# One-hot tiles for the score passes of a graph network: built on VectorE from row numbers, or transposed once, stored and loaded

## The reference

```
x = _layernorm(x + _L0_gnn_ref(x, edge_index, edge_attr_64, ...), axis=-1)   # three attention layers, 4 heads
x = _layernorm(x + _L1_gnn_ref(x, edge_index, edge_weight, ...), axis=-1)    # two graph convolutions
x = _layernorm(x + _L2_gnn_ref(x, edge_index, ...), axis=-1)                 # one graph convolution
x = _layernorm(x + _L3_gnn_ref(x, src, dst, ...), axis=-1)                   # two mean-aggregation layers
```

```
logits = jax.nn.leaky_relu(a_s[src] + a_d[dst] + ew[:, None], NEG_SLOPE)
m = jax.ops.segment_max(logits, dst, num_segments=n)
ex = jnp.exp(logits - m[dst])
```

## Time and profile before

| | |
|---|---|
| time, 3 runs | 5626.39, 5626.62, 5635.58 us; median 5626.62 |
| profiled execution | span 5076.4 us from its first to its last instruction; median less span is 550.2 us |
| busy share of the span | PE 77%, DVE 75%, ACT 68%, POOL 59% |
| transfers | 1061.18 MB, 209 GB/s over the span |
| score passes | `delta` from 1251.5 to 1611.3, 2041.6 to 2327.3, 2753.6 to 2933.5 and 2959.6 to 3085.1 us |

### The profile page before, as it was taken

The page is one execution under the profiler, slowest core; times in us unless marked ns, Lnnn a source line. Parts: engine busy times, 40 slices in busy tenths (PEclk is TensorE's granted clock), DMA queues, the critical chain, the costliest instruction groups (busy, mean ns, idle before and its releaser), DMA issues. The chain is left out here.

```text
span 5076.4 us, 107540 instructions
## 1 busy us (share of the span) xinstructions
PE 3921.6 (77%) x23992; PEld 2865.7 (56%) x23992; DVE 3818.0 (75%) x14850; ACT 3446.1 (68%) x11317; POOL 3017.8 (59%) x2914
## 2 busy tenths in 40 slices
PE   2999999565997798994998974997876676665554
PEld 1666766344775455773555752444765565665554
DVE  5899999676998787887886966997768787444443
ACT  0899999554886576784776863887878787333332
POOL 2888888475552122661223452887757676767777
PEclk9999999788998899997999997998999898997666
DMA  2566666587997576994776984775766566543332
GB/s 63 162 186 199 199 194 193 175 288 242 351 349 250 180 239 205 338 354 160 233 241 230 350 290 156 225 227 171 230 205 212 189 204 190 155 145 116 93 101 70
DMA packets 606699, 1061.18 MB, mean 209 GB/s; under 512 B 109737, under 2 KB 130875, under 8 KB 606509
## 3 DMA queue, kind: packets, MB, share of 16 engines
q1 hardware_dynamic: 524780, 920.61, 53.0%
q0 software_dynamic: 81728, 138.51, 10.7%
HBM read 608.75 MB, written 453.92 MB: 209 GB/s over the span
## 5 line engine op out<-in xcount | busy, mean ns | idle before, releaser
L2534 POOL DMA_INDIRECT got_c<-table,src_row x980 | 930.4, 949 | 387.6 <-issue 295.6
L1428 POOL DMA_INDIRECT src_got_s<-table,src_row x588 | 554.6, 943 | 452.9 <-PE bank L1474 105.1
L2566 PE MATMUL bank<-pick_c,got_c 128*128 128x128 f32 x1960 | 327.7, 319 | 349.6 <-DMA got_c<-table,src_row 271.2
L2076 PE MATMUL bank<-w_all,dt_m 128*128 128x512 f32 x1176 | 567.7, 599 | 35.0 <-DMA dt_m<-delta_t 33.4
L2566 PEld LDWEIGHTS bank<-pick_c,got_c 128*128 128x128 f32 x1960 | 284.2, 223 | 392.5 <-issue 233.5
L2050 POOL TENSOR_TENSOR part_m<-part_m,half_sum_m 128x512 f32<-128x512 f32 x98 | 158.7, 1619 | 580.3 <-DVE half_sum_m L2283 580.3
L1601 ACT ACTIVATE z_s<-z_s,shift_s,dev_s 128x128 f32<-128x128 f32 x1080 | 444.2, 486 | 1.8 <-DVE shift_s L1739 1.3
L791 PEld LDWEIGHTS bank<-w_mean,ht 128*128 128x128 f32 x2352 | 312.4, 193 | 142.9 <-issue 142.9
L2590 PE MATMUL bank<-w_c,agg_c 128*128 128x128 f32 x1960 | 365.4, 311 | 5.0 <-ACT agg_c L2711 4.7
L2711 ACT COPY agg_c<-bank 128x512 f32<-128x512 f32 x245 | 142.6, 582 | 325.4 <-DVE bank L1914 277.8
L788 PE MATMUL bank<-bias,first_row 128*128 128x512 f32 x588 | 321.8, 629 | 38.7 <-ACT ht L851 13.8
(11 more groups left out here) (352 smaller groups left out, 11925.4 us busy)
## 6 DMA issues: line engine op xcount, KB each, us to landing
table<-rows SPq DMA_DIRECT2D x294, 256.0 KB
x_s<-table SPq DMA_DIRECT2D x270, 256.0 KB
x_c<-table SPq DMA_DIRECT2D x245, 256.0 KB
table<-z_s SPq DMA_DIRECT2D x196, 256.0 KB
table<-z_c SPq DMA_DIRECT2D x196, 256.0 KB
table<-mid_s SPq DMA_DIRECT2D x172, 256.0 KB
own_rows_s<-table SPq DMA_DIRECT2D x147, 256.0 KB
pick_t_s<-picks_t SPq DMA_DIRECT2D x147, 256.0 KB
```

The costliest lines, as they stand in the source:

```text
L1428: nc.gpsimd.indirect_dma_start(out=src_got[r][:, g, :], out_offset=None, in_=tables[l].rows, in_offset=bass.IndirectOffsetOnAxis(ap=src_ro ...
L2076: nc.tensor.matmul(b_h[k % n_h][:, :], dt[b.slot][:, k, :], w_all[:, l, :, :].rearrange("p h d -> p (h d)"), start=True, stop=True).then_i ...
L2534: nc.gpsimd.indirect_dma_start(out=got[r][:, g, :], out_offset=None, in_=t_in.rows, in_offset=bass.IndirectOffsetOnAxis(ap=src_row[:, t:t ...
L2566: ins = nc.tensor.matmul(b_sum[r][:, k * P:(k + 1) * P], got[b.slot][:, k, :], pick[r][:, k, :], start=k == 0, stop=sage, skip_group_check ...
```

## The change

The transposed one-hot tiles are no longer made from `pick` by TensorE and ScalarE, nor stored, nor loaded. In `edge_structure` VectorE writes the keys of all slots as bytes; SyncE stores them in one row of 25088 bytes and loads that row into all 128 partitions (`keys`, 25088 bytes a partition, kept to the end). A new input, `row_of`, holds each partition's number. In every step of `edge_scores` VectorE makes `pick_t` of a batch with one instruction, which compares 512 bytes of `keys` with `row_of`. `pick_t` has two buffers instead of four. GpSimd's pacing in the slot pass waits for `pick` instead of the transposed tile.

```diff
-        picks_t = nc.dram_tensor("picks_t", (nb * P, GB * P), F32, kind="Internal").ap()
+        key_row = nc.dram_tensor("key_row", (1, n_slots), U8, kind="Internal").ap()
...
+        row_of = sb("row_of", [P, 1])
+        keys = sb("keys", [P, n_slots], U8)
+        keys_in = ctx.enter_context(nc.semaphore("keys_in"))
...
-                n_load = 13
+                n_load = 14
...
                         sp.dma_start(iota[:, :], io["iota"]).then_inc(loaded, 16)
+                        sp.dma_start(row_of[:, :], io["row_of"]).then_inc(loaded, 16)
                         sp.dma_start(wet[:, :, :], io["L0_gnn_We"].rearrange("l e h -> e l h")).then_inc(loaded, 16)
                         sp.dma_start(bem[:, :, :], io["be_all"]).then_inc(loaded, 16)
                         sp.wait_ge(iotas, 3)
                         sp.dma_start(row_map.rearrange("(p r) f -> p (r f)", p=P),
                                      map_def[:, :, :].rearrange("p r f -> p (r f)")).then_inc(map_out, 16)
+                        sp.wait_ge(keys_made, 1)
+                        sp.dma_start(key_row[0, :].rearrange("(q e) -> q e", q=rq), key_bytes[:, :]).then_inc(keys_out, 16)
+                        sp.wait_ge(keys_out, 16)
+                        sp.dma_start(keys[:, :], key_row.to_broadcast([P, n_slots])).then_inc(keys_in, 16)
                         sp.wait_ge(map_out, 16)
...
                         st(nc.vector.tensor_tensor(kr[:, :], kr[:, :], sr[:, :], ALU.add))
+                        nc.vector.tensor_copy(key_bytes[:, :], kr[:, :]).then_inc(keys_made, 1)
...
                                 sp.wait_ge(ht_made, b.count(1, 1))
                                 sp.sem_inc(sp_pace, 1)
                                 sp.dma_start(turned_batch(state_t[0], b), ht[r][:, :]).then_inc(ht_stored[r], 16)
-                                sp.wait_ge(pick_t_made, b.count(1, 1))
-                                sp.sem_inc(sp_pace, 1)
-                                sp.dma_start(turned_batch(picks_t, b), pick_t[r][:, :]).then_inc(pick_t_stored[r], 16)
...
                                 elif b > 5 and g == 3:
-                                    pool.wait_ge(pick_t_made, b - 4)
+                                    pool.wait_ge(pick_made, b - 3)
...
                                 nc.tensor.matmul(bank[1][:, :], w_first[:, :], xt[b.half][:, :], start=True,
                                                  stop=True).then_inc(h_made, 1)
-                                pe.wait_ge(pick_made, b.count(1, 1))
-                                hold(pe, pick_t_made, b.count(1, 0))
-                                for g in range(GB):
-                                    ins = nc.tensor.transpose(bank[4][:, g * P:(g + 1) * P], pick[b.slot][:, g * P:(g + 1) * P], ident[:, :])
-                                ins.then_inc(picks_turned, 1)
...
                                 nc.scalar.activation(ht[b.slot][:, :], hidden[r][:, :], ACT.Identity,
                                                      bias=beta_col[:, 0:1]).then_inc(ht_made, 1)
-                                act.wait_ge(picks_turned, b.count(1, 1))
-                                hold(act, pick_t_stored[b.slot], b.ring4(16, -16))
-                                nc.scalar.copy(pick_t[b.slot][:, :], bank[4][:, :]).then_inc(pick_t_made, 1)
...
                                 hold(dve, pick_stored[b.slot], b.ring4(16, -16))
-                                hold(dve, picks_turned, b.count(1, -1))
                                 for k in range(GB):
...
-                src_got, own_rows, pick_t, dt = (fours(n) for n in ("src_got", "own_rows", "pick_t", "dt"))
-                delta = pairs("delta")
+                src_got, own_rows, dt = (fours(n) for n in ("src_got", "own_rows", "dt"))
+                delta, pick_t = pairs("delta"), pairs("pick_t")
...
-                        def load_picks(b):
-                            hold(sp, spread_made, b.count(1, -3))
-                            sp.sem_inc(sp_pace, 1)
-                            sp.dma_start(flat(pick_t[b.slot]), turned_batch(picks_t, b, start)).then_inc(pick_in[b.slot], 16)
...
                         def loads(b):
                             load_own(b)
-                            load_picks(b)
                             if not early(b):
...
                             pe.wait_ge(own_in[r], b.ring4(16))
-                            pe.wait_ge(pick_in[r], b.ring4(16))
+                            pe.wait_ge(picks_made, b.count(1, 1))
                             if first:
                                 hold(pe, dt_made, b.count(1, 0))
                             else:
                                 hold(pe, delta_made, b.count(1, 0))
                             for g in range(GB):
-                                ins = nc.tensor.matmul(b_spread[:, g * D:(g + 1) * D], pick_t[r][:, g, :], own_rows[r][:, g, :],
+                                ins = nc.tensor.matmul(b_spread[:, g * D:(g + 1) * D], pick_t[b.half][:, g, :], own_rows[r][:, g, :],
                                                        start=True, stop=True, skip_group_check=True)
                             ins.then_inc(spread_made, 1)
...
                         dve.wait_ge(banks_open, len(set_by_dve))
+                        dve.wait_ge(keys_in, 16)
...
+                        def build_picks(b):
+                            hold(dve, spread_made, b.count(1, -1))
+                            dve.sem_inc(dve_pace, 1)
+                            nc.vector.tensor_scalar(flat(pick_t[b.half]), keys[:, bass.ds((b.batch() + start) * (GB * P), GB * P)],
+                                                    row_of[:, 0:1], None, ALU.is_equal).then_inc(picks_made, 1)
 
...
                         def step_two(at):
+                            b = at(0)
+                            if b:
+                                build_picks(b)
                             b = at(1)
                             if b:
                                 moments(b, 0)
...
                                 moments(b, 1)
                             b = at(0)
                             if b:
+                                build_picks(b)
                                 residual(b, 0)
                             b = at(1)
                             if b:
...
                                 residual(b, 0)
                                 middle(b, 0)
                                 moments(b, 0)
+                            b = at(0)
+                            if b:
+                                build_picks(b)
                             b = at(1)
                             if b:
                                 set_bias(b, 0)
...
+        "row_of": _np.arange(P, dtype=_np.float32).reshape(P, 1),
```

19 lines of the change are left out of this document (11 added, 8 removed).

## The result

The changed kernel takes 5652.24 us (median of 11 runs, 5641.83 to 5659.17) beside 5640.23 us for the kernel before (11 runs, 5626.39 to 5647.69). The ratio is 1.0025, 95% interval 1.0014 to 1.0035, so +8 to +20 us. The prediction was 5675, +48.5. The direction is right and the size is not: about a quarter of it came. 5652.24 does lie inside the stated range of 5648 to 5710, but by luck: the kernel before measured 13.6 us more in 11 runs than in the three from which the prediction started.

A forecast was written before the change was run, and what follows sets the result against it. VectorE was taken to limit passes 1 to 3 and a VectorE-TensorE loop pass 4; 20.6 + 10.5 + 10.8 + 7.8 - 2 (slot pass) + 0.8 (start) = +48.5, so 5626.6 -> 5675 us, range 5648 to 5710.

The forecast's parts named there:

- The difference, 550.2 us: Whole kernel: median run 5626.6 us minus profiled span 5076.4 us, taken as time outside the span and left unchanged.
- pass 1: First score pass, 49 batches, two-layer order: VectorE is the limit, so each build adds 0.42 us, +20.6 us.
- pass 2: Second score pass, 49 batches, one-layer order: VectorE alone would need 6.11 us against 5.95 a batch, +7.8 us.
- pass 3: Third score pass, 25 batches, two-layer order: VectorE is the limit, 0.42 us a build, +10.5 us.
- pass 4: Fourth score pass, 24 batches, solo order: build lies inside a VectorE-TensorE loop, 0.45 us each, +10.8 us.
- the surplus for collisions and for the register step: Added to the build's 0.40 us: 0.02 for GpSimd collisions, and in pass 4 0.03 for register step and semaphore.
- Loads taken away in passes 1, 3 and 4: Removed 256 KB one-hot loads: nobody waits for them in the steady part, so they give nothing.
- the stall: In pass 2, ScalarE's 33.3 us wait for the score store; 12.6% less traffic ends it, with no further relief.
- A: Build reads bytes at one element a cycle, 0.62 us each: together +78 us, 5704 us; chance 0.12.
- B: VectorE and GpSimd block each other during builds: +32 us more at most, 5707, priced at half, 5690; chance 0.08.
- C: Memory traffic bounds the score passes, so removed loads give -112 us, 5515 us; chance of faster, all forms, 0.05.
- D: Build hides in idle VectorE time of passes 2 and 4; passes 1 and 3 pay 25 us, 5650; chance 0.10.

The follow-up runs named there:

- The slot pass alone: Kernel before without the slot pass's transposes, ScalarE copy and store, untransposed one-hots loaded instead; -3.6, -6.4 and -8.2 us in three sessions.
- the build alone: Kernel before with the byte row and an unused build added, loads and slot pass kept; +45.1, +47.0 and +42.3 us in three sessions.

## Why the prediction was wrong in size

**The step that failed** is the first one: "The difference, 550.2 us, lies outside the span, and I carry it unchanged." In every profiled execution of this study where the two stand side by side, 1.7 to 3.0 us lie around the span. The trace was of an execution near 5080 us, the timed runs of some near 5630. Everything was priced on passes of which the timed runs have only 1 and 3, and those but for their starts. Whether that trace and the three timed runs beside it were taken in one session isn't known.

**In the condition of the trace** the sum holds up: forecast +48.5, measured +41.2. First to last `delta`, changed minus before near 5088 (traces of two sessions): pass 1 +19.0 (forecast 20.6), pass 2 +6.3 (7.8), pass 3 +9.6 (10.5), pass 4 +9.5 (10.8). 19.0 / 48 = 0.40 us a build in pass 1 and 9.5 / 23 = 0.41 in pass 4, where 0.42 and 0.45 were forecast: the surplus for collisions and for the register step was too high or not needed. The slot pass alone gave 4 to 8 us instead of 2.

**In the condition of the timed runs** two terms were wrong. "Loads taken away in passes 1, 3 and 4 ... give nothing" and in pass 2 nothing beyond the stall: near 5640 all the loads give 20.3 us together. And near 5690 the builds cost 30.0 us instead of 49.7. Passes 1 and 3 pay them in full there, 0.44 and 0.43 us a batch away from their ends (74 x 0.43 = 32 us), and passes 2 and 4 only 0.06 and 0.17, because VectorE no longer sets them (7.13 and 6.95 us a batch in the kernel before, against the 5.95 and 5.46 on which their terms stood). That is read from one trace of each kernel. From first to last `delta` the same two traces differ by 44 us in the four passes, but their own times also lie 47 us apart, 17 more than the medians. From one session, -15.8 for the removed work and +30.0 for the builds make the +14.2.

**The rivals.** A (a byte read at one element a cycle) is out: 480 ns. The Trainium skill ("VectorE: DVE Perf Modes", section "What auto-detection actually checks") asks, for two elements a cycle, for a single source and a destination in SBUF, with outermost dimensions both even or equal, and for no width of the type; this trace agrees, 512 byte columns in 480 ns where a 128x512 copy from PSUM takes 680. B (VectorE and GpSimd block each other) is out: the longest of 147 builds is 698 ns, half of them last 480 or less, and their mean is 496, so that all surpluses together are some 2 us. C (memory traffic) is out in its strong form: pass 1 kept VectorE's limit, and the removed loads are worth 20 us near 5640 and not 112. Whether those 20 are traffic at all is open. D (the build hides) holds for most of passes 2 and 4 near 5690, and is wrong near 5088, where the build alone costs 42 to 47 us. That D's 5650 is close to the 5652 measured is the luck told above.

**What would have shown it.** The build's row, pass 1's waits, TensorE's 93% and the 295 GB/s came as announced. The first gather of pass 1 did not: 1294.9 in the compared profile against 1239.3, 56 us later, because the slot pass, which had lost work, took longer than in the trace of before. That no edit explains. Inside one session, near 5690, the change brings this gather forward, from 1315.1 to 1307.3.

**What stays open.** Why SyncE's instructions take 0.7 us in some sessions is not known, nor whether they are the cause of the late transfers or suffer from the same thing. In the trace of the kernel before near 5690 the slot pass has 70 of them (among 627 such instructions), pass 2 has 37 of 922, the convolution 115 of 1610, and pass 1 has 13 of 1112; that is a coincidence in place and no proof. The slot pass alone and the build alone were run only near 5088. Their share near 5640 is inferred from the other runs.

## What to carry to other kernels

Set the span of the profiled execution against the timed runs before pricing anything. If they differ by more than a few us on one core, the trace is of another condition, and every term but those of a stage with an engine at its limit needs a second value. Here that would have kept passes 1 and 3 (+31) and put a question mark on the rest. Compare rises with rises: a time can fall into a forecast range because the kernel before was measured again and came out higher.

A new instruction costs what it occupies in the stage whose limit its engine is, and one may hand it to an engine with room even if it occupies that one four times as long: 1.58 us on GpSimd cost less than 0.40 us on VectorE in passes 1 and 3. Near 5088 it cost more in passes 2 and 4, where four gathers leave GpSimd a microsecond or less.

## What the runs showed of the hardware

- A 128x512 one-hot build from bytes with a per-partition operand takes 480 ns on VectorE and occupies 0.40; on GpSimd 1584 ns.
- One kernel, one core: 5088 us in some sessions and 5640 to 5690 us in others, on one chip even both. Pass 1 and the stages between the passes keep their length (pass 1 359.9 and 361.9 us; 430.6 in both from its last `delta` to the first of pass 2); the slot pass (249 to 306), pass 2, pass 4 and the convolution grow, and pass 3 at its start. In the longer executions some 3% of SyncE's register and semaphore instructions (289 of 8618) last 0.68 to 0.74 us, where 0.03 is usual.
